# The steps that prepare each unit of h, spread over six pieces of the matrix

## The reference

```python
h = jnp.maximum(_layernorm(x, axis=-1), 0.0)      # eps 1e-5
out = x + (1.0 - 0.1) * (adj @ h) + 0.1 * h0
```

## Time and profile before

| | before |
|---|---|
| median of 3 runs | 710.65 us (710.53 to 710.77) |
| time of the profiled execution | 710.53 us |
| its span in the profile | 708.4 us |
| TensorE (PE) busy | 703.5 us, 99% of the span |
| VectorE (DVE) busy | 634.5 us, 90% |
| ScalarE (ACT) busy | 531.8 us, 75% |
| GpSimd (POOL) busy | 26.8 us, 4% |
| DMA | 285.74 MB, mean 403 GB/s |
| TensorE's granted clock | 1.00 of full speed throughout (2.4 GHz) |

### The profile page before, as it was taken

The page is one execution under the profiler, slowest core; times in us unless marked ns, Lnnn a source line. Parts: engine busy times, 40 slices in busy tenths (PEclk is TensorE's granted clock), DMA queues, the critical chain, the costliest instruction groups (busy, mean ns, idle before and its releaser), DMA issues.

```text
span 708.4 us, 8165 instructions
## 1 busy us (share of the span) xinstructions
PE 703.5 (99%) x3086; PEld 577.8 (82%) x3086; DVE 634.5 (90%) x549; ACT 531.8 (75%) x463; POOL 26.8 (4%) x38
## 2 busy tenths in 40 slices
PE   9999999999999999999999999999999999999998
PEld 5878888888888888888888888888888888888886
DVE  4999999999999999999898888888988898889885
ACT  4899998788788787887776767676767676767673
POOL 1100000000000000000000000000000000000000
PEclk9999999999999999999999999999999999999999
DMA  9999999999999999999999999999999999999990
GB/s 364 419 418 418 419 419 416 419 418 416 421 415 418 420 417 419 417 417 422 417 402 415 407 412 384 382 399 412 413 421 405 423 420 422 421 421 422 414 412 20
DMA packets 46550, 285.74 MB, mean 403 GB/s; under 512 B 5168, under 2 KB 9520, under 8 KB 14000
## 3 DMA queue, kind: packets, MB, share of 16 engines
q1 hardware_dynamic: 46080, 283.99, 97.8%
q10 hardware_dynamic: 432, 1.25, 0.5%
HBM read 281.02 MB, written 4.19 MB: 403 GB/s over the span
## 4 chain that ended last, share of the span: by engine, by line
PE 94%; DMA 3%; DVE 1%; ACT 1%; SPq 0%; issue 0%; DVEq 0%
PE acc L457 16%; PE acc L453 16%; PE acc L452 16%; PE acc L436 15%; PE acc L441 15%; PE acc L430 15%; DMA raw<-wide_dram 3%; DVE a_lo L345 1%; ACT a_hi L301 0%; SPq L213 0%; SPq L196 0%; DVE stats L311 0%; ACT h_full L271 0%; DVE mean_var L321 0%; SPq L226 0%
## 5 line engine op out<-in xcount | busy, mean ns | idle before, releaser
L345 DVE TENSOR_TENSOR a_lo<-raw,a_hi 128x2048 fp32r<-128x2048 f32 (+1 forms) x292 | 582.4, 2010 | 58.1 <-ACT a_hi L301 57.1
L301 ACT ACTIVATE a_hi<-raw 128x2048 fp32r<-128x2048 f32 (+1 forms) x368 | 497.9, 1382 | 160.6 <-PE acc L457 100.1
L452 PE MATMUL acc<-a_hi,h_hi 128*128 128x512 f32 x512 | 199.2, 389 | 0.0
L453 PE MATMUL acc<-a_hi,h_lo 128*128 128x512 f32 x512 | 199.2, 389 | 0.0
L430 PE MATMUL acc<-a_hi,h_hi 128*128 128x512 f32 x504 | 167.9, 390 | 0.0
L436 PE MATMUL acc<-a_hi,h_lo 128*128 128x512 f32 x504 | 167.6, 389 | 0.1
L457 PE MATMUL acc<-a_lo,h_hi 128*128 128x512 f32 x512 | 136.8, 389 | 0.0
L441 PE MATMUL acc<-a_lo,h_hi 128*128 128x512 f32 x504 | 135.2, 389 | 0.1
L453 PEld LDWEIGHTS acc<-a_hi,h_lo 128*128 128x128 f32 x512 | 96.1, 188 | 20.0
L457 PEld LDWEIGHTS acc<-a_lo,h_hi 128*128 128x128 f32 x512 | 96.1, 188 | 19.9
L452 PEld LDWEIGHTS acc<-a_hi,h_hi 128*128 128x128 f32 x512 | 96.1, 188 | 19.9
(11 more groups left out here) (15 smaller groups left out, 30.5 us busy)
## 6 DMA issues: line engine op xcount, KB each, us to landing
raw<-tall_dram SPq DMA_DIRECT2D x128, 1024.0 KB, 8.3
raw<-wide_dram SPq DMA_DIRECT2D x126, 1024.0 KB, 11.1
res_sb<-res_dram SPq DMA_DIRECT2D x16, 512.0 KB, 9.9
x_sb<-x_dram SPq DMA_DIRECT2D x30, 128.0 KB, 11.1
out_dram<-finished SPq DMA_DIRECT2D x15, 256.0 KB, 8.5
raw<-early_dram ACTq DMA_DIRECT2D x2, 512.0 KB, 6.7
raw<-early_dram SPq DMA_DIRECT2D x2, 512.0 KB, 5.9
out_dram<-finished SPq DMA_DIRECT2D x2, 128.0 KB, 1.8
```

The lines of the kernel that those rows point to most:

```text
L301: nc.scalar.activation(a_hi[:, q % SPLIT_SLOTS, cols], raw[:, q % RAW_SLOTS, cols], ACT.Copy).then_inc(hi_ready, 1)
L345: nc.vector.tensor_tensor(a_lo[:, q % SPLIT_SLOTS, cols], raw[:, q % RAW_SLOTS, cols], a_hi[:, q % SPLIT_SLOTS, cols].bitcast(fp32), ALU.s ...
L452: nc.tensor.matmul(bank, h_hi[:, k, :], a_hi[:, slot, cols], start=(k == 0), stop=False)
L453: nc.tensor.matmul(bank, h_lo[:, k, :], a_hi[:, slot, cols], start=False, stop=False)
```

## The change

The two sets of distances, for early and for later units, become one. For a unit due at piece d: both statistics stand at d - 6 on VectorE, aggregate (with eps) at d - 4, shift at d - 3, scale at d - 2, high and low h at d - 1. The x load stands at d - 5 for all units. No instruction is added or removed, and nothing else in the kernel differs.

```diff
-LATE = 16
 LOAD_X_AT = {}
 STATS_AT, AGGREGATE_AT, SHIFT_AT = {}, {}, {}
 SCALE_AT, HIGH_H_AT = {}, {}
 for _u in range(1, len(UNITS)):
     _a = UNITS[_u][0]
     _due = QUADS * _a
-    if _a < LATE:
-        LOAD_X_AT[_due - 5] = _u
-        STATS_AT[_due - 5] = [_a, _a + 1]
-        AGGREGATE_AT[_due - 5] = SHIFT_AT[_due - 4] = _u + 1
-        SCALE_AT[_due - 2] = _u
-    else:
-        LOAD_X_AT[_due - 6] = _u
-        STATS_AT[_due - 6] = STATS_AT.get(_due - 6, []) + [_a]
-        STATS_AT[_due - 5] = [_a + 1]
-        AGGREGATE_AT[_due - 5] = SHIFT_AT[_due - 4] = _u + 1
-        SCALE_AT[_due - 2] = _u
-    HIGH_H_AT[_due - 1] = _u
+    LOAD_X_AT[_due - 5] = _u
+    STATS_AT[_due - 6] = [_a, _a + 1]
+    AGGREGATE_AT[_due - 4] = SHIFT_AT[_due - 3] = _u + 1
+    SCALE_AT[_due - 2] = HIGH_H_AT[_due - 1] = _u
```

## The result

| | before | after |
|---|---|---|
| median | 710.39 us (710.15 to 710.77, 13 runs) | 711.92 us (711.37 to 712.54, 13 runs) |
| profiled span | 708.4 us | 709.8 us |
| GpSimd busy | 26.8 us | 72.0 us |

The ratio is 1.002, with a 95% interval of 1.0013 to 1.0028: slower by 1.5 us, where +1.4 us was forecast (712.0, on the 710.65 us of the first three runs). Microsecond figures of single steps come from one profiled execution of each kernel.

What follows compares the result with a forecast made beforehand. TensorE was taken as the bound at 2.72 us a piece, with 0.95 us lost before piece 13. Waits of 2.18 less 0.74 won made +1.4 on 710.65: 712.0 us, range 710.7 to 713.1.

Steps and rivals of the forecast that it cites:

- The start: Up to piece 13, moved statistics, aggregate and eps free a_lo and low h: 0.74 us won, bounds 0.4 and 0.95.
- what piece 9 gives back: At piece 9 a_lo still ends at 34.53, so of the 0.36 us won at piece 4 only 0.15 survive.
- x a piece later: x loads behind a later piece; some 4 us cover it, cost nothing; rival of late x: 712.3, 1%.
- Pow: GpSimd's pow, started during the long a_lo behind eps, ends 0.55 us behind it: 2.7 us in some 20 rows.
- remainder: GpSimd: the time pow still takes after the VectorE instruction that held it ends, 0.55 us.
- The loop: One unit of four pieces, a_lo in front of shift to the next: 10.91 us against TensorE's 10.88, no reserve; 86%.
- drift: In the late units' loop, lateness grows by 0.03 us a unit, 0.54 over some 18 units.
- Seeds: Residual sums behind pieces 45 to 115 bring lateness: 4 x 0.60 behind low h, 4 x 0.37 behind shift, together 3.88.
- Sum: TensorE waits 2.18 us from about piece 80 to 123, less 0.74 won at the start: +1.4 us, 712.0.
- The near tie: First units: pow and a_lo start 0.02 us apart; if pow wins, lateness begins at piece 55, 0.36 to 0.5 less.

Runs made afterwards that it cites:

- e7: Changed kernel with the first eight residual sums twelve pieces apart from piece 47 on, seven in the loop behind low h: 712.33 us, ratio 1.0031.
- e1: Changed kernel with the new distances only for units due before piece 44, the old ones for the rest: 709.62 us, ratio 0.9993.
- e8: Changed kernel with x loaded at due-6 again for the units that had it there before: 711.95 us, ratio 1.0023.
- e3: Changed kernel with the a_lo between eps and shift (pieces 41, 45, ..., 121) in two halves: 709.37 us, ratio 0.9989.
- e4: Changed kernel with one useless short VectorE subtraction directly behind eps in each unit of two blocks: 709.40 us, ratio 0.9987.
- e10: Changed kernel with shift a piece later (due-2) and scale a piece later (due-1, in front of high h): 710.07 us, ratio 0.9998.
- e5: Changed kernel with only the first residual sum behind a piece of the loop (45), the others from piece 125 on: 709.72 us, ratio 0.9991.
- e6: Changed kernel with the first eight residual sums twelve pieces apart from piece 45 on, seven in the loop behind shift: 710.48 us, ratio 1.0003.

## Why the prediction was right

**The start.** Forecast -0.74, with bounds of -0.4 and -0.95. The count of TensorE's starts up to piece 13 went from 0.95 to 0.05 us, -0.90, less 0.08 that piece 2 began later in that execution. The term that was off is what piece 9 gives back: I had 0.21 us there, since its a_lo would end at 34.53 as before. Its data landed some 0.2 us earlier (30.76 against 30.96) and only 0.03 were lost, at piece 10. That is chance in part: e7 has the same tables for these pieces, and in its profiled execution 0.36 were lost at pieces 9 and 10. e1, the start alone, is 0.7 below before.

**x a piece later.** Nothing, as forecast; e8 shows it. In the kernel after, one x landed 0.35 us behind its piece (128.02 and 127.67).

**Pow.** Forecast: 2.7 us in some 20 rows; there are 21, with a median of 2.68. Its remainder behind VectorE's instruction is 0.55 to 0.56 behind a half, a whole a_lo and low h alike. e3 and e4 show it to be a cause of the loss: each leaves the steps in their places and shortens pow, by what stands directly behind eps, and the loss goes. e10 shows the other half: with pow as long as ever but shift a piece later, the loss goes too. By the Trainium skill (SBUF — State Buffer, "Who interferes with whom") the order of issue decides which of the two engines stands still. The traces agree for GpSimd as the second to issue. For VectorE as the second they do not: in e5 an a_lo that started 0.03 behind pow took 2.31 us, 0.02 more than the others and not 0.7, and in the changed kernel half an a_lo that started at 31.97, 0.47 behind a pow of 0.70, took 1.22 as ever.

**The loop.** Forecast 10.91 us; the unit above has 10.90. The terms had added up to 10.87, just under TensorE's 10.88, and 0.04 was put on top because instructions that had to wait showed 0.01 more. In the unit above they do: a_lo 2.29, pow's remainder 0.56, the hand-over to ScalarE 0.04, the h_full pair 0.78. The sign of the drift hung on such hundredths, so that it came out is luck in part. In e5, where nothing else enters, the time by which a_lo lags behind its a_hi grows from 0.06 to 0.41 between pieces 53 and 121, 0.02 a unit. I had taken 0.03.

**Seeds.** 0.60 behind low h and 0.37 behind shift; in the changed kernel the margin of a_lo of pieces 53 and 57 (on both sides of the sum at 55) falls from 2.29 to 1.67, that of 65 and 69 from 1.63 to 1.26: 0.60 and 0.35 beside 0.02 of drift. The margin is the time from a_lo's end to the start of its first product. e6 and e7 show that the branch decides.

**Sum.** 2.18 us of stalls were forecast from about piece 80 to 123; 2.10 were counted from piece 86 to 124. What the sum did not have is the 0.11 us at piece 128, where the same lateness reaches `finished`. Where the errors are (start 0.16 too little, stalls 0.08 too much, 0.11 and 0.08 not seen) they nearly cancel, which is luck for the total but not for the terms.

**The near tie.** The prediction left open who wins when pow and a_lo start within 0.02 us. In the changed kernel a_lo was first in every late unit, by 0.02 in the first, so lateness began at piece 45. Over all traces an a_lo that came first by 0.005 us or more held pow, and a pow that came first by 0.03 or more was not held. The start alone does not decide closer than that: once in e3 both rows start at 181.27, pow 0.003 ahead, and pow was held (GpSimd, then VectorE):

```profile
181.27 1.78 POOL L255 TENSOR_TENSOR rstd<-var_eps,exponent 128x2 f32<-128x2 f32 x1 [9.04 <-DVE var_eps L315]
...
181.27 2.36 DVE L336 TENSOR_TENSOR a_lo<-raw,a_hi 128x1024 fp32r<-128x1024 f32 x2
```

The kernels e3 (709.37) and e4 (709.40) beat both: before by 0.9 us (0.13%), the changed one by 2.5. Of the 0.95 us that there was to win, they have nearly all.

## What to carry to other kernels

A helper engine that is idle 96% of the time can still set the end, if its one short instruction must get in between long two-input instructions of VectorE: look at which instruction stands directly behind the one that releases it, and let it be a short one (0.28 us in e4) or a split one (e3). Before a step with a wait is moved, add up the closed path over one period, with the waits in it, against the bottleneck's period: a path equal to it costs nothing by itself, but loses the power to recover, and any extra work in it later is paid in full once the slack is used up. And follow on which branch of such a path the extra work stands, since only what exceeds the parallel branch counts (0.36 of 0.60 here).

## What was not expected of the hardware

The order of two starts 0.01 to 0.03 us apart made pow 0.70 us or 2.84 us long in one execution (e5). It held in one direction only: a pow that came first lengthened the a_lo behind it by some 0.02 us at most.

And a pow that is held gets in between two of VectorE's instructions although the second starts 0.08 us before the first ends. In the kernel before, the pow at 29.21 was held by the low h that ends at 29.47; this row stands behind it on VectorE:

```profile
29.38 2.35 DVE L345 TENSOR_TENSOR a_lo<-raw,a_hi 128x1024 fp32r<-128x1024 f32 x2
```

Pow ended at 30.01, 0.55 behind low h, and didn't wait for the first half of this a_lo, which ends at 30.60. That is why low h behind eps, and a split a_lo in e3, leave pow short.
